# K's norms through a signed selection matrix, the mask in 64x32 tiles, the feed-forward's layer norm in its own bank, Q's even quads first

## What is computed

```python
for i in range(DEPTH):                                  # 6 layers
    x = attn_layer(shift_tokens(x), Wqkv[i], q_scale[i], k_scale[i], Wo[i]) + x
    x = ffn_layer(shift_tokens(x), ln_g[i], ln_b[i], W1[i], b1[i], W2[i], b2[i]) + x

def attn_layer(x, Wqkv, qs, ksc, Wo):                   # 16 heads of 64
    q, k, v = split(x @ Wqkv)
    q = l2norm(q) * qs                                  # t / max(|t|, 1e-12)
    k = l2norm(k) * ksc
    q = q * cos * scale + rotate_half(q) * sin * scale
    k = k * cos / scale + rotate_half(k) * sin / scale
    # windows of 32 queries see their own 32 keys and the 32 before
    sim = where(mask, -max, einsum(bq, bk2) * 8)
    return (softmax(sim) @ bv2) @ Wo

def ffn_layer(x, g, bln, W1, b1, W2, b2):
    xn = (x - mu) / sqrt(var + 1e-5) * g + bln
    a, gate = split(xn @ W1 + b1)                       # 341 each
    return a * gelu(gate) @ W2 + b2
```

## Time and profile before

| | us |
|---|---|
| median of 3 runs | 1750.26 |
| lowest, highest | 1747.34, 1756.39 |
| span of the profiled execution, first to last instruction | 1764.5 |
| PE busy in it | 1603.1 (91%) |
| DVE busy | 1226.0 (69%) |
| ACT busy | 1147.8 (65%) |
| POOL busy | 1002.6 (57%) |

### The profile page before, as it was taken

The page is one execution under the profiler, slowest core; times in us unless marked ns, Lnnn a source line. Parts: engine busy times, 40 slices in busy tenths (PEclk is TensorE's granted clock), DMA queues, the critical chain, the costliest instruction groups (busy, mean ns, idle before and its releaser), DMA issues. The chain is left out here.

```text
span 1764.5 us, 75677 instructions
## 1 busy us (share of the span) xinstructions
PE 1603.1 (91%) x33590; PEld 1308.3 (74%) x33590; DVE 1226.0 (69%) x1912; ACT 1147.8 (65%) x2115; POOL 1002.6 (57%) x757
## 2 busy tenths in 40 slices
PE   5969899988999999999998999998999999999987
PEld 4557778777777777777787787787777777778765
DVE  7766677675767767767776776776777677677662
ACT  2246677765676776766776677676676676767644
POOL 2155566664656666655675665685566585566551
PEclk9989999998999999999999999999999999999987
DMA  3266665675566567566657656657665665665650
GB/s 129 57 168 136 156 151 131 155 182 132 126 150 155 123 154 204 139 143 154 141 135 184 167 129 152 150 128 184 164 148 133 161 143 137 157 155 123 150 123 25
DMA packets 98567, 252.96 MB, mean 143 GB/s; under 512 B 30016, under 2 KB 36288, under 8 KB 97472
## 3 DMA queue, kind: packets, MB, share of 16 engines
q1 hardware_dynamic: 98240, 248.12, 59.1%
HBM read 44.59 MB, written 2.10 MB: 26 GB/s over the span
## 5 line engine op out<-in xcount | busy, mean ns | idle before, releaser
L803 DVE SCALAR_TENSOR_TENSOR UV<-ps,veca,rope 128x512 f32<-128x512 f32 x768 | 530.7, 744 | 187.5 <-PE ps L381 163.7
L1210 POOL TENSOR_TENSOR KK<-UV 128x512 f32<-128x512 f32 x192 | 241.6, 1280 | 396.3 <-DVE UV L803 393.0
L955 ACT ACTIVATE sq<-ps 128x512 f32<-128x512 f32 (+1 forms) x400 | 228.1, 583 | 269.5 <-PE ps L381 176.8
L1210 POOL TENSOR_TENSOR Qtb<-UV 128x512 f32<-128x512 f32 x192 | 243.1, 1288 | 92.4 <-DVE UV L803 92.4
L381 PE MATMUL ps<-xh,wh 128*128 128x256 f32 x768 | 244.4, 318 | 4.4 <-DVE UV L803 2.5
L381 PEld LDWEIGHTS ps<-PT,V 64*64 64x64 f32 x12288 | 199.1, 137 | 45.0 <-issue 38.6
L1229 POOL TENSOR_TENSOR E<-E,ri 128x1024 f32<-128x1024 f32 x96 | 182.7, 1903 | 78.6 <-DVE ri L876 73.2
L381 PE MATMUL ps<-PT,V 64*64 64x32 f32 x12288 | 215.7, 222 | 8.0 <-issue 5.0
L381 PE MATMUL ps<-xh,wl 128*128 128x256 f32 x768 | 217.1, 283 | 0.9 <-issue 0.9
L381 PE MATMUL ps<-xl,wh 128*128 128x256 f32 x768 | 217.2, 283 | 0.0
L1220 POOL TENSOR_TENSOR E<-E,mx 128x1024 f32<-128x1024 f32 x96 | 182.7, 1903 | 58.6 <-DVE mx L870 58.6
(11 more groups left out here) (128 smaller groups left out, 3113.9 us busy)
## 6 DMA issues: line engine op xcount, KB each, us to landing
V<-Vs SPq DMA_DIRECT2D x672, 128.0 KB
KK<-KK SPq DMA_DIRECT2D x384, 128.0 KB
Qtb<-Qtb SPq DMA_DIRECT2D x384, 128.0 KB, 2.4
rope<-in_c_rope SPq DMA_DIRECT2D x48, 512.0 KB
raw<-in_Wqkv SPq DMA_DIRECT2D x6, 1536.0 KB, 7.8
V<-Vs SPq DMA_DIRECT2D x96, 64.0 KB
V<-V SPq DMA_DIRECT2D x96, 64.0 KB, 2.0
wo<-in_Wo SPq DMA_DIRECT2D x6, 512.0 KB
```

Of the source, the lines that this page charges most:

```text
L803: e.scalar_tensor_tensor(UV[:, p % 2, slot, :].rearrange("p (i t) -> p i t", i=2), ps[:, half, :].rearrange("p (i t) -> p i t", i=2), veca ...
L955: return e.activation(out, in_, f, **kw)
L1210: e.tensor_tensor(dst, u, v, op).then_inc(s["rot_done"], 1)
```

## The change

Six things are changed.

- `a_rl` moves from POOL to DVE and computes something else: Rhl = R * is_low - Rh. `is_low` is 1 in the upper 16 partitions of each quad and 0 in the lower; so the lower 16 rows hold -Rh, the upper ones R - Rh. For this `ind` repeats each head's column in both places, and `sel` has -1 at the lower and +1 at the upper, so that one product gives Rh + (R - Rh). `a_sp` is now two 128x128 products for each bank, four in all in place of eight; it goes by bank and not by half, and each half of `a_kn` waits for its own bank alone.
- In the list `a_rl` moves from behind `a_sqy1` to behind `b_max1`. On DVE it stands between the second row maximum and `c_zn`.
- The mask is eight products in 64x32 tiles with `identb` everywhere; `fourb` and its two copies are gone.
- The layer norm of the feed-forward (`c_mu`, `c_zsq`, `c_var`, `c_rs`, `c_zn`) uses bank FF; `c_mu` takes over the wait for the previous `c_fin` (`xa_done`) from `c_h`. The second `b_pt` waits for the residual `xb_done` in place of `zn_done`.
- `queries` issues quads 0, 2, 1, 3, with one semaphore for the even and one for the odd; the first four heads of `b_s` wait for the even, the next four for the odd.
- The clamps no longer wait for `rl_done`.

```diff
-    b_sub0 b_s0 a_rot1 b_nrm0 a_sqx0 a_mx1 b_s1 a_my1 a_x1 a_y1 c_xb a_sqy1 a_rl c_wo w_h0 b_s2 b_sum0 b_sub1
+    b_sub0 b_s0 a_rot1 b_nrm0 a_sqx0 a_mx1 b_s1 a_my1 a_x1 a_y1 c_xb a_sqy1 c_wo w_h0 b_s2 b_sum0 b_sub1
...
-    mask = np.where(np.stack([first, seen, np.roll(first, W, 0)], 1), 0.0, NEG)
+    mask = np.where(np.stack([first, seen, np.roll(first, DH, 0)], 1), 0.0, NEG)
-            sel[W * q + hq, q, hq * W:(hq + 1) * W] = 1
+        for row, sign in ((hq, -1), (W // 2 + hq, 1)):
+            ind[hq * W:(hq + 1) * W, row] = 1
+            for q in range(HQ):
+                sel[W * q + row, q, hq * W:(hq + 1) * W] = sign
+    ind[:, W] = a >= W // 2
...
-                for hq in range(HQ):
+                for hq in (0, 2, 1, 3):
...
-                                    Qt[hq * W:(hq + 1) * W, half, :, :]).then_inc(s["q_in"], 16)
+                                    Qt[hq * W:(hq + 1) * W, half, :, :]).then_inc(s[("qe_in", "qo_in")[hq % 2]], 16)
...
-            def a_sp(m, i):
-
-                if i:
-                    e.wait_ge(s["rkb_done"], m * 2 + 1)
+            def a_sp(m, b):
+
+                if b:
+                    e.wait_ge(s["mul_done"], m * 16 + (12 if m else 8))
                 else:
-                    e.wait_ge(s["rl_done"], m + 1)
-                for x in range(2):
-                    for b in range(2):
-                        if x == 0 and i == 0 and b == 0:
-                            e.wait_ge(s["sq_done"], m * 8 + (6 if m else 4))
-                        elif x == 0 and i == 0:
-                            e.wait_ge(s["mul_done"], m * 16 + (12 if m else 8))
-                        q = 2 * b + i
-                        rows = slice(q * W, (q + 1) * W)
-                        ins = mm(ps[:, b, i * T:(i + 1) * T], sel[rows, q, :], (Rh, Rl)[x][rows, :], x == 0, x == 1,
-                                 tile_position=(q * W, 0))
+                    e.wait_ge(s["rhl_done"], m + 1)
+                    e.wait_ge(s["sq_done"], m * 8 + (6 if m else 4))
+                for i in range(2):
+                    ins = mm(ps[:, b, i * T:(i + 1) * T], sel[:, 2 * b + i, :], Rhl[:, :])
                 ins.then_inc(s["rkb_done"], 1)
...
-                        if chosen:
-                            rows = slice(r * DH, r * DH + W)
-                            mm(ps[:, 2 + r, :].rearrange("p (j k) -> p j k", j=HP), fourb[rows, :],
-                               mask[rows, 1:2, :].broadcast_to([W, HP, KEYS]), True, False, skip_group_check=True,
-                               tile_position=(r * DH, 0))
-                            continue
+                        rows = slice(r * DH, (r + 1) * DH)
                         for w in range(NW):
+                            v = 2 * r if first and w == 0 else 1
+                            mm(ps[w * W:(w + 1) * W, 2 + r, :].rearrange("p (j k) -> p j k", j=HP), identb[rows, r * DH:r * DH + W],
+                               mask[rows, v:v + 1, :].broadcast_to([DH, HP, KEYS]), True, False, skip_group_check=True,
+                               tile_position=(r * DH, w * W))
                 if i == 0:
-                    e.wait_ge(s["q_in"], n * 128 + 128)
+                    e.wait_ge(s["qe_in"], n * 64 + 64)
+                elif i == 1:
+                    e.wait_ge(s["qo_in"], n * 64 + 64)
...
                 elif n:
-                    e.wait_ge(s["zn_done"], n)
+                    e.wait_ge(s["xb_done"], n * C)
...
                 e.wait_ge(s["z_act"], j * 2 + 2)
-                mm(ps[:, WO, 0:T], cen[:, :], zs[:, :]).then_inc(s["mu_done"], 1)
+                e.wait_ge(s["xa_done"], G + j)
+                mm(ps[:, FF, 0:T], cen[:, :], zs[:, :]).then_inc(s["mu_done"], 1)
...
+            def a_rl(m, _):
+
+                e.wait_ge(s["rh_done"], m + 1)
+                if m:
+                    e.wait_ge(s["rkb_done"], m * 2)
+                e.scalar_tensor_tensor(Rhl[:, :], R[:, 0, :], is_low, Rh[:, :], ALU.mult,
+                                       ALU.subtract).then_inc(s["rhl_done"], 1)
+
             def a_kn(m, b):
 
-                e.wait_ge(s["rkb_done"], m * 2 + 2)
+                e.wait_ge(s["rkb_done"], m * 2 + b + 1)
...
-            def a_rl(m, _):
-
-                e.wait_ge(s["rh_done"], m + 1)
-                e.tensor_tensor(Rl[:, :], R[:, 0, :], Rh[:, :], ALU.subtract).then_inc(s["rl_done"], 1)
```

More of the change, by code:

```diff
@@ L111, in constants @@
     first = seen & ~((np.arange(P)[:, None] < W) & (kk[None, :] < W))
-    mask = np.where(np.stack([first, seen, np.roll(first, W, 0)], 1), 0.0, NEG)
-    ind = np.zeros((P, W), f32)
+    mask = np.where(np.stack([first, seen, np.roll(first, DH, 0)], 1), 0.0, NEG)
+    ind = np.zeros((P, W + 1), f32)
     sel = np.zeros((P, HQ, P), f32)
     for hq in range(HQ):
-        ind[hq * W:(hq + 1) * W, hq] = 1
-        for q in range(HQ):
-            sel[W * q + hq, q, hq * W:(hq + 1) * W] = 1
+        for row, sign in ((hq, -1), (W // 2 + hq, 1)):
[3 more added lines that the diff above has]
+    ind[:, W] = a >= W // 2
     blk = (np.arange(P)[:, None] // DK == np.arange(P)[None, :] // DK).astype(f32)
@@ L177, in program @@
         Rh = sb("Rh", [P, T], F32R)
-        Rl = sb("Rl", [P, T], F32R)
+        Rhl = sb("Rhl", [P, T], F32R)
         rq = sb("rq", [P, C, HQ, HQ])
@@ L189, in program @@
         identb = sb("identb", [P, P], BF16)
-        fourb = sb("fourb", [P, P], BF16)
         ident = sb("ident", [P, P])
-        ind = sb("ind", [P, W])
+        ind = sb("ind", [P, W + 1])
+        is_low = ind[:, W:W + 1]
         sel = sb("sel", [P, HQ, P], F32R)
@@ L515, in b_s @@
                     e.wait_ge(s["x1_done"], G1)
-                chosen = 0 if n % G == 0 and c == 0 else 1
+                first = n % G == 0 and c == 0
                 if i % 2 == 0:
@@ L740, in _ @@
             e.tensor_copy(identb[:, :], ident[:, :]).then_inc(s["sel_done"], 1)
-            for r in range(2):
-                rows = slice(r * DH, r * DH + W)
-                e.tensor_copy(fourb[rows, :].rearrange("p (g k) -> p g k", g=NW),
-                              ident[rows, rows].unsqueeze(1).broadcast_to([W, NW, W])).then_inc(s["sel_done"], 1)
             e.tensor_scalar(cen[:, :], ident[:, :], -1.0 / D, None, ALU.add).then_inc(s["sel_done"], 1)
@@ L827, in clamp @@
                 e.wait_ge(s["norm_done"], step * 2 + side + 1)
-                if step and side == 0:
-                    e.wait_ge(s["rl_done"], step)
-                elif step:
+                if step and side:
                     e.wait_ge(s["rqt_done"], step)
@@ L940, in _ @@
             m_add(2)
+            a_rl(0, 0)
             a_kn(0, 0)
@@ L946, in _ @@
             m_add(3)
-            run({"a_mx": a_mx, "a_my": a_my, "a_rck": a_rck, "b_rcq": b_rcq, "a_kn": a_kn, "b_rq": b_rq, "b_scale": b_scale,
+            run({"a_mx": a_mx, "a_my": a_my, "a_rck": a_rck, "a_rl": a_rl, "b_rcq": b_rcq, "a_kn": a_kn, "b_rq": b_rq, "b_scale": b_scale,
                  "b_max": b_max, "b_sum": b_sum, "b_xb": b_xb, "c_xb": c_xb, "c_zn": c_zn,
@@ L1105, in c_zsq @@
                 e.wait_ge(s["mu_done"], j + 1)
-                act(zq[:, :], ps[:, WO, 0:T], ACT.Square).then_inc(s["zsq_done"], 1)
+                act(zq[:, :], ps[:, FF, 0:T], ACT.Square).then_inc(s["zsq_done"], 1)
             def c_rs(j, _):
                 e.wait_ge(s["var_done"], j + 1)
-                act(zr[:, :], ps[:, WO, T:2 * T], ACT.Ln, bias=eps[:, 0:1]).then_inc(s["zln_done"], 1)
+                act(zr[:, :], ps[:, FF, T:2 * T], ACT.Ln, bias=eps[:, 0:1]).then_inc(s["zln_done"], 1)
                 e.wait_ge(s["zln_done"], j + 1)
@@ L1203, in a_rot @@
                 if m and p % 2 == 0:
-                    e.wait_ge(s["k_in" if p == 0 else "q_in"], m * 128)
+                    if p == 0:
+                        e.wait_ge(s["k_in"], m * 128)
+                    else:
+                        e.wait_ge(s["qe_in"], m * 64)
+                        e.wait_ge(s["qo_in"], m * 64)
                 q = 2 * (p % 2)
@@ L1234, in _ @@
             a_rot(0, 1)
-            a_rl(0, 0)
             a_rot(0, 2)
-            run({"b_nrm": b_nrm, "w_l": w_l, "c_wl": c_wl, "c_zl": c_zl, "a_xl": a_xl, "a_halo": a_halo, "a_rot": a_rot, "a_rl": a_rl, "b_sub": b_sub},
+            run({"b_nrm": b_nrm, "w_l": w_l, "c_wl": c_wl, "c_zl": c_zl, "a_xl": a_xl, "a_halo": a_halo, "a_rot": a_rot, "b_sub": b_sub},
                 lambda g: None)
```

24 lines of the change are left out of this document (9 added, 15 removed).

## The result

The changed kernel takes 1732.1 us (median of 4, 1727.7 to 1734.6), the kernel before 1751.8 beside it: a ratio of 0.987, 95% interval 0.984 to 0.991. In a second set of runs it was 1729.1 and a ratio of 0.984 (0.981 to 0.987). The forecast of 1734 us was met as a time. As a gain it was too small: 16 us were forecast, and 20 (first set) and 27 (second set) were measured. The experiments show that the terms behind it did not hold: two of them were wrong in opposite directions.

What follows compares the result with a forecast made beforehand. PE was taken as near the bound, merely keeping up with the other engines before the projection. Q 11 + selection and layer norm 5 + prologue 0.4 = 16 us off the profiled 1764.5, less 0.8%: 1734 us, range 1720 to 1760.

Steps and rivals of the forecast that it cites:

- 5 us gained by selection and layer norm: Row maximum to output projection: all edits there, Rhl's delay included, gain 0.1 us a pass, 5 us (-5 to +14).
- Q's quads: Start of the scores: the first half waits only for the even quads' copies, 11 us gained (4 to 16).
- Layer norm in bank 7: Second softmax transposes: the 0.52 us wait for zs goes, at most 0.05 comes through, counted as nothing.
- Rhl at 0.40 us on DVE: Between row maximum and zs on DVE: Rhl takes 0.40 us (0.35 to 0.45), putting ACT's work 0.34 later.
- the second regime: From the output projection on, PE runs without a wait up to the next pass's first scores.
- Selection by one product: Around a_sp: PE's work up to the projection shrinks by 0.6 us a pass, nearly all of it hidden.
- Mask, 0: Masks before the scores: eight products take 0.3 us, as the two did, so nothing is gained.
- the rival of queued tiles: Masks before the scores: only two of eight products run at once, 0.92 us for 0.32, 1757 us; chance 0.05.
- POOL first: After the row maximum: POOL's subtraction gets SBUF before Rhl, zs and its followers 1.9 us later, 1822 us; chance 0.11.
- Wrong if the wait for Q keeps its 23.9 us.: Sign for PE's wait for Q's copies: it should fall from 23.9 to about 12 us, else the prediction is wrong.

Runs made afterwards that it cites:

- run 12: Not a run's number: the sentence counts 12, not 13, shorter waits for Q's copies in the middle of the profiled run of the kernel before.
- rhl_pool_pto1: The changed kernel with Rhl back on POOL in two steps, and ACT's second copy of PT ahead of zs's bias and zh: 1721.1 us (1722.2 without that move).
- sel_only: The kernel before with only the selection by one product and Rhl on DVE: 1772.2 us, ratio 1.0072.
- rl_twice: The changed kernel with a second step like Rhl, into a tile nobody reads, ahead of it on DVE in each pass: 1915.7 us, ratio 1.0900.

## Why the prediction was right, point by point

The time was near by luck, because two wrong terms partly cancelled: 11 us for Q's order, which is worth 15 alone and 33 in its place, and 5 us gained by selection and layer norm, which with the mask cost 6. Together that is a gain of 27 us where 16 were forecast.

- **Q's quads, 11 us (4 to 16).** Alone 15 us, with the wait at 12.7 where I had said about 12. In the changed kernel the term was mis-sized threefold, since I took the 26 waits of before for fixed. The same change makes 40 of them, and long ones. The text said that the wait would fall to 12; it fell to 19.4 and 23.0, from 44. There is also a slip in the sum: of the 24 waits in the middle of the run 12, not 13, are the shorter ones, 0.32 us on average, which leaves the term at 11 to 12 us.
- **Layer norm in bank 7, 0.** Right alone (1.0002). The wait for PT was foreseen at 0.2 to 0.5 us (0.30 and 0.46 in a pass), and to shorten it gains nothing (rhl_pool_pto1). Beside the selection it may be worth more: sel_only, in which the transposes stand 40.1 us for zs, loses 15 us, and with layer norm and mask added the loss is 6. No kernel takes it alone out of the changed one.
- **Rhl at 0.40 us on DVE.** Its length (0.48, of which 0.09 overlap) and the delay of ACT were right in kind (0.34 said, 0.28 measured), and so was the projection, 4.73 us behind the row maximum where 4.7 was forecast. The step that failed is the next one. The prediction looked for what Rhl delays up to the projection and stopped there. "In the second regime PE runs without a wait up to the next pass's first scores" holds for PE, but the delay of ACT goes on: exponential, OT, hid, the second scaling of K, K's copies, Q's copies. K's copies get the 0.28 us whole and Q's last one 0.38 in sel_only and 0.19 in the changed kernel, while PE comes 0.2 us earlier and meets them. Instead of gaining 0.11 us a pass, the part alone loses 0.29 (33.71 to 34.00).
- **Selection by one product.** PE's own time shrank as costed (0.62 us on average in sel_only). The changes of tiling that it saves were hidden, as held: by ACT up to c_fin, which ends only 0.22 earlier, and for that rest by the copies.
- **Mask, 0.** Right as far as the runs can tell. Eight products in 64x32 tiles need 0.23 us up to the scores, so they run at once, and the rival of queued tiles is out.
- **POOL first, +72 us, chance 0.11.** It did not happen, for the reason given (DVE is 0.16 us ahead). rl_twice made it happen: its mechanism and its 0.28 us were exact, but the price would have been nearer the 187 us of rl_twice than 83, an estimate from its nearly equal delay (2.04 us) and PE's lower clock behind the stall.
- **"Wrong if the wait for Q keeps its 23.9 us."** It nearly did (19.4, and 23.0 in the second set), with the time as forecast. A sum of waits isn't a term that stays put while the rest changes.

## What to carry to other kernels

When two rings close on the same instruction, shortening one moves the wait to the other: for each instruction added to an engine, follow what it delays, over the other engines and the copies, to the next pass, and not only to the next product. Take a part out of the finished kernel as well as putting it alone into the old one, since here the same edit was worth 15 us and 33. An engine that stands idle in the right microsecond (POOL, 1.4 us ahead of its subtraction) takes even two instructions without delaying anything in the pass shown, where one on the engine that hands work on costs 7 us.
